# Four contiguous additions in the place of one strided sum at the end of a tile

## The reference

```python
    for W in filters:                      # f0, f1, f2
        z = jnp.einsum('bfd,bgd->bfgd', x0, xk).reshape(b, f * g, d)
        cur = jnp.einsum('bpd,pm->bmd', z, W)
        outs.append(cur)
        xk = cur
    return jnp.sum(jnp.concatenate(outs, axis=1), axis=-1)
...
    e = jnp.stack([tbl_0[ids[:, 0]], ..., tbl_38[ids[:, 38]]], axis=1)
    h = jnp.concatenate([z, dense_ctx], axis=1)
    h = jnp.maximum(h @ W_top1 + b_top1, 0.0)
    h = jnp.maximum(h @ W_top2 + b_top2, 0.0)
    y = h @ W_top3
```

## Time and profile before

| | |
|---|---|
| median of 3 runs | 777.85 us (773.94, 777.85, 781.08) |
| span of the profiled execution | 775.4 us |
| its time beside the runs | the span is 2.5 us below their median |
| mean granted TensorE clock | 0.985 of full speed |
| busy ACT | 536.4 us (69%) |
| mean share of DMA traffic | 40.27 MB, 52 GB/s |

### The profile page before, as it was taken

The page is one execution under the profiler, slowest core; times in us unless marked ns, Lnnn a source line. Parts: engine busy times, 40 slices in busy tenths (PEclk is TensorE's granted clock), DMA queues, the critical chain, the costliest instruction groups (busy, mean ns, idle before and its releaser), DMA issues.

```text
span 775.4 us, 12234 instructions
## 1 busy us (share of the span) xinstructions
PE 658.1 (85%) x2571; PEld 471.9 (61%) x2571; DVE 687.4 (89%) x1110; ACT 536.4 (69%) x1862; POOL 509.0 (66%) x462
## 2 busy tenths in 40 slices
PE   0768888898989888898989898878989898998988
PEld 0246656566766666666766675656666666666563
DVE  1448899999999999999999999979999998999880
ACT  2055768496876767686859686665859696788672
POOL 6755868586767767685868676766868644455340
PEclk9899999999999999999999999998999999999999
DMA  7540404040412214040404031220404041300200
GB/s 190 109 103 6 102 2 100 7 97 8 86 18 54 51 23 82 2 103 1 98 7 96 9 82 23 46 53 7 98 7 96 9 106 31 97 2 1 64 1 0
DMA packets 57049, 40.27 MB, mean 52 GB/s; under 512 B 35455, under 2 KB 39885, under 8 KB 57032
## 3 DMA queue, kind: packets, MB, share of 16 engines
q1 hardware_dynamic: 51206, 38.73, 22.4%
q0 software_dynamic: 5120, 1.29, 1.9%
q10 hardware_dynamic: 706, 0.06, 0.1%
HBM read 38.13 MB, written 1.94 MB: 52 GB/s over the span
## 4 chain that ended last, share of the span: by engine, by line
PE 40%; DMA 18%; issue 17%; DVE 16%; POOL 4%; SPq 2%; ACT 2%; DVEq 1%; ACTq 0%; POOLq 0%
DMA pairs<-x_rows 17%; DVE parts L486 7%; PE psd L769 5%; PE psa L769 4%; PE psa L773 4%; PE psa L770 4%; PE psd L773 4%; PE psd L770 3%; DVE z0l L442 3%; PE ps L728 2%; DVE pairs L435 2%; PE psg L747 2%; PE ps L721 2%; POOL parts L379 1%; ACT prods L618 1%
## 5 line engine op out<-in xcount | busy, mean ns | idle before, releaser
L618 ACT ACTIVATE prods<-psa,x0c 128x128 f32<-128x128 f32 x1024 | 296.8, 393 | 60.5 <-PE psa L773 52.8
L459 DVE TENSOR_REDUCE cur<-parts 128x128 f32<-128x2048 f32 x64 | 245.8, 3840 | 4.1 <-POOL parts L379 3.9
L486 DVE SCALAR_TENSOR_TENSOR parts<-psd,x0c,parts 128x128 f32<-128x128 f32 x704 | 194.3, 342 | 6.4 <-PE psd L773 6.4
L379 POOL TENSOR_TENSOR parts<-parts,prods 128x512 f32<-128x512 f32 x128 | 167.9, 1311 | 40.5 <-ACT prods L618 39.0
L769 PE MATMUL psa<-w1h,x1h 128*128 128x512 f32 x384 | 173.8, 453 | 9.9 <-ACT prods L618 8.8
L346 POOL DMA_INDIRECT emb<-tables,idx x140 | 146.5, 1047 | 32.1 <-issue 19.3
L769 PE MATMUL psd<-w1h,x1h 128*128 128x512 f32 (+1 forms) x256 | 112.6, 440 | 50.0 <-DVE parts L486 48.0
L773 PE MATMUL psa<-w1h,x1l 128*128 128x512 f32 x384 | 152.6, 397 | 0.0
L770 PE MATMUL psa<-w1l,x1h 128*128 128x512 f32 x384 | 152.4, 397 | 0.0
L379 POOL TENSOR_TENSOR parts<-prods 128x512 f32<-128x512 f32 x64 | 84.1, 1313 | 99.2 <-ACT prods L618 89.8
L618 ACT ACTIVATE parts<-psa,x0c 128x128 f32<-128x128 f32 x512 | 143.3, 422 | 2.3 <-ACT x1f L565 2.2
(11 more groups left out here) (87 smaller groups left out, 753.3 us busy)
## 6 DMA issues: line engine op xcount, KB each, us to landing
pairs<-x_rows SPq DMA_DIRECT2D x30, 546.0 KB
pairs<-x_rows SPq DMA_DIRECT2D x15, 468.0 KB
x0t<-x_rows SPq DMA_DIRECT2D x16, 234.0 KB
emb<-tables,idx POOLq DMA_INDIRECT x140
pairs<-x_rows SPq DMA_DIRECT2D x8, 156.0 KB
x_rows<-emb SPq DMA_DIRECT2D x14, 72.0 KB
wt_sb<-w_top SPq DMA_DIRECT2D x1, 768.0 KB, 12.1
prods<-w SPq DMA_DIRECT2D x1, 704.0 KB, 4.8
```

The lines of the kernel that those rows point to most:

```text
L379: pool.tensor_tensor(parts[:, t % 2, 1, :], first, prods[:, p % P_RING, :], ALU.add).then_inc(pool_adds, 1)
L459: dve.tensor_reduce(cur1[:, t % 2, :], parts[:, t % 2, :, :].rearrange("p k (j m) -> p m (k j)", m=M), AX.X, ALU.add).then_inc(c1_ready, 1)
L486: op = dve.scalar_tensor_tensor(acc, y[:, M * j:M * j + M], x0c[:, t, GF * g + j:GF * g + j + 1], acc, ALU.mult, ALU.add)
L618: op = act.activation(dst[:, M * j:M * j + M], y[:, M * j:M * j + M], ACT.Copy, scale=x0c[:, t, GF * g + j:GF * g + j + 1])
```

## The change

In `finish_tile` the one `tensor_reduce` over sixteen values with a stride of 128 is replaced by four `tensor_tensor` additions on the same engine. The 2048 columns are taken as one row; the first adds the upper 1024 to the lower 1024 in place, the second 512 to 512, the third 256 to 256, and the fourth writes 128 + 128 to `cur1`. A new semaphore `halved` makes each wait for the one before. The place of `finish_tile` in DVE's queue, the three waits ahead of it and all other engines' instructions are as before; the order of the numbers in the floating-point sum is another.

```diff
@@ -236,6 +236,7 @@
+        halved = sem("halved")
@@ -456,9 +457,15 @@
 
                 if not isinstance(T, int) or T >= 2:
                     dve.wait_ge(g2_done, T - 1)
-                dve.tensor_reduce(cur1[:, t % 2, :],
-                                  parts[:, t % 2, :, :].rearrange("p k (j m) -> p m (k j)", m=M),
-                                  AX.X, ALU.add).then_inc(c1_ready, 1)
+                own = parts[:, t % 2, :, :].rearrange("p k n -> p (k n)")
+                n = (2 + DIRECT) * GF * M // 2
+                for k in range(3):
+                    if k:
+                        dve.wait_ge(halved, 3 * T + k)
+                    dve.tensor_tensor(own[:, 0:n], own[:, 0:n], own[:, n:2 * n], ALU.add).then_inc(halved, 1)
+                    n //= 2
+                dve.wait_ge(halved, 3 * T + 3)
+                dve.tensor_tensor(cur1[:, t % 2, :], own[:, 0:n], own[:, n:2 * n], ALU.add).then_inc(c1_ready, 1)
```

## The result

The changed kernel takes 839.38 us in the median (835.95 to 840.28), against 777.88 us before (four runs of each). The ratio is 1.078, with a 95% interval of 1.073 to 1.082: **7.8% slower**. The profiled execution has a span of 838.4 us.

The account below looks back on a forecast made before the run. DVE sets the pace. Per block, 6.4 us waiting against 2.7 clean gain, less 0.7 slack, gives +3.0; fourteen blocks add 42 to 775.4, making 817; with 2.5 for the median, rounded up, 821 us. Range 758 to 860.

Parts of the forecast that it names:

- the clean gain: Four undisturbed additions against L459 at a tile's end on DVE: 0.68 us less per tile, 2.7 us per block.
- The wait on the own engine: Gap before each of three additions waiting for the one before on DVE: 0.20 us, from the last L459 behind L486.
- the prediction's other end: Clean chain with neighbours overlapping by 0.10 us everywhere: 2.17 us, 1.58 less than L459; with the waiting, 778 us.
- The waiting for POOL: Additions in the four tile ends of a block held by POOL's tensor instructions: together 6.4 us per block.
- A: Tile end with L459 at 388.57: the 1024 wide addition waits 2.56 us for three POOL instructions.
- the first rival: Much slower: the chains run into x0d and the addition behind it, up to 877 us; chance 0.18.
- B: Tile end with L459 at 398.64: the 512 wide addition waits about 1.30 us for POOL's addition at 399.54.
- D: Tile end with L459 at 419.93: the 512 wide addition waits for POOL's addition at 420.78, 1.29 us long.
- C: Tile end with L459 at 411.14: the 512 wide addition waits for POOL's addition at 412.40, 1.29 us long.
- The slack: DVE's idle pieces of 0.46 us ahead of L474 and 0.21 us ahead of L435 take up 0.7 us per block.
- The second rival: Faster: additions fall into POOL's pauses or start first, 758 us, or 735 if the transfer moves forward; chance 0.18.
- The third, no change: Gaps between additions below 0.1 us, or half of the collisions with POOL dodged: 770 to 785 us; chance 0.14.

Follow-up runs that it names:

- the pair with POOL emptied: POOL's additions and x0d replaced by one-column instructions plus zero fills, in the changed kernel (714.95 us) and in the kernel before (742.64 us).
- the emptied kernel: The changed kernel with POOL's additions and x0d replaced by one-column instructions plus zero fills: 714.95 us, ratio 0.916 to the kernel before.

## Why the prediction was right, point by point

**The mechanism was right.** That the additions have two SBUF inputs, that POOL's reading instructions hold them, and that this outweighs the clean gain is shown by the pair with POOL emptied: the same edit of POOL in both kernels turns the sign. The forecast of 821 us was 18 us below the 839 measured, inside the range. That it came so near is in part luck, as two of its sizes, the second and third points below, were off in opposite directions.

**The clean durations** were 1.21, 0.68, 0.41 and 0.27 us by interpolation and are 1.21, 0.69, 0.43 and 0.29 in the emptied kernel.

**The wait on the own engine** was taken at 0.20 us from the earlier trace rows and is 0.8 us of idle in 24 tiles, 0.03 us each. That row was a poor stand-in: L459 there stands at the end of the program and behind three waits. The clean chain is 2.65 us, not 3.07, and the clean gain 1.1 us per tile, not 0.68 (4.5 us in a block, not 2.7). Of the two ends, 0.20 us and an overlap of 0.10, I chose the one slightly farther off. The rule of the Trainium skill that I weighed there (VectorE: DVE Perf Modes, The DRAIN you can't avoid: a semaphore behind each instruction costs nothing) is nearer to the 0.03 us. Such a chain gives up one more thing, the overlap of 0.10 us that neighbours without a wait have in the records, so it does not reach the 2.17 us of the prediction's other end.

**The waiting for POOL** was taken at 6.4 us per block and is 9.4: (118.9 - 24 x 2.61) / 6, with 2.61 the sum of the least durations. This term and the one above were off in opposite directions, by 3.0 and by 1.8 us in a block, so that they partly cancelled. Its places were partly wrong. The 2.56 us on the 1024 wide addition in A did not come: its mean is 1211 ns, and POOL's first addition now follows its start (388.61 after 387.70 above), where it came before it. I had laid the new chain over POOL's old times; that POOL would move was only a word in the rivals. Instead the 128 wide addition at the end waits 1.27 us in the mean, for x0d and the addition behind it. That is what the first rival said of the tails, in two ends of tiles out of four (2.51 us in B and 2.46 in D, against 0.29 in C and 0.69 in A), though the rival had put the most of it in C.

**From the first addition to the instruction behind the last** I gave 5.6 us in A and 4.4 in the others, 4.7 in the mean. It is 5.84 (B), 3.62 (C), 5.78 (D) and 4.01 (A): 4.8 in the mean, so the mean was right and the places were wrong.

**The slack** of 0.7 us per block in DVE's idle pieces did not give: the idle time ahead of L481 grew from 4.4 to 6.4 us in six blocks. A block rose by 4.6 us where I had 3.0: the additions are +4.8 and not +3.7, the slack of 0.7 did not help and the idle time grew by 0.3, L436 and L450 took 0.8 more, and L443 gave back 1.4, which I had counted only as part of an end. The slack and the two sizes above are the steps that were off. The block was also 42.0 us before, not the 41.4 of my count of 29 sums in 300 us.

**The second rival**, faster, had its mechanism right and its condition unmet: with POOL emptied the additions gain 28 us, where I had 20, and the waits for the transfer of `pairs` and for PE's products take the rest. The third, no change, did not come, though its premise of small gaps did.

TensorE's mean granted clock is 0.941 of full speed in the profiled run and 0.985 before. Whether this cost anything was not tried. DVE's idle time ahead of L481 and L493, where it takes up PE's products, rose by 2.5 of the 27.7 us in six blocks, so a slower PE can have made DVE wait directly for no more than that.

## What to carry to other kernels

Before cutting one instruction of the busiest engine into several faster ones, look at how many of the new ones another engine can hold, and at what that engine does in the same microseconds. Here each two-input addition on VectorE behind the first cost 0.45 to 1.3 us of waiting for GpSimd, and the smallest one the most. Keeping the widest step as an addition and leaving the rest to one reduction took 1.8% off. Collisions that are driven out of one place by a wait come back in another.

## What the runs showed of the hardware that was not expected

- GpSimd's fills with zeros do not hold two-input instructions of VectorE (1215, 692, 426 and 293 ns beside fills of 530 ns), its additions and x0d, which read SBUF, do (1308, 874 and 1559 ns for the last three, in the mean).
- GpSimd pays too when it comes second: POOL's first addition of a tile, which mostly falls on the 1024 wide addition that is never held there, takes 1607 ns in the mean in the changed kernel from 200 to 500 us (41.8 us for 26), and 1321 ns before (38.3 us for 29).
- A write with a stride of four float32 costs about 0.8 ns per element more on VectorE (444 against 343 ns for 128, 1072 against 682 for 512) and 1.0 ns on ScalarE (522 against 392 for 128); the 444 ns include a read with the same stride. A read with a stride of 128 about 0.8 ns more than runs of four (3846 against 2260 ns for 2048).
- One VectorE instruction can wait for two of GpSimd's in a row, and can be held by one that is recorded up to 0.40 us behind its own start (391.11 and 391.51 above).
